# Graph propagation with residual LayerNorm: the scaling of the degrees and of z moved from VectorE to GpSimd

## The reference, cut to what matters

```python
# x: (8, 2048, 64), W = adj: (8, 2048, 2048), U: (2048, 16), w_scale: scalar
Ws = 0.5 * (W + swapaxes(W, -1, -2))
A = sigmoid(U @ U.T)
K = Ws * A
deg = maximum(K.sum(axis=-1), 1e-12)
d = rsqrt(deg)
y = w_scale * einsum('bnm,bmc->bnc', K * d[:, :, None] * d[:, None, :], x)
out = layernorm(x + y)
```

## Time and profile before

| | |
|---|---|
| median of 3 runs | 464.87 us (460.85 to 467.07) |
| the profiled execution's own time | 463.4 us |
| its span in the trace | 461.6 us |
| PE busy | 433.8 us, 94% |
| DVE busy | 412.7 us, 89% |
| ACT busy | 207.8 us, 45% |
| POOL busy | 116.8 us, 25%, 134 instructions |
| one batch, steady | about 52.4 us |

### The profile page before, as it was taken

The page is one execution under the profiler, slowest core; times in us unless marked ns, Lnnn a source line. Parts: engine busy times, 40 slices in busy tenths (PEclk is TensorE's granted clock), DMA queues, the critical chain, the costliest instruction groups (busy, mean ns, idle before and its releaser), DMA issues.

```text
span 461.6 us, 14416 instructions
## 1 busy us (share of the span) xinstructions
PE 433.8 (94%) x5302; PEld 227.9 (49%) x5302; DVE 412.7 (89%) x1153; ACT 207.8 (45%) x655; POOL 116.8 (25%) x134
## 2 busy tenths in 40 slices
PE   7887999999998999999999999999999999999993
PEld 6555444554444544554445544554445544555341
DVE  6988777999899988999899989999899998999645
ACT  3797332654254433553426442554426543454311
POOL 0000000013340334203340234203340234303444
PEclk9999899999999999999999999999999999999997
DMA  8999699988999799998999999998999999996012
GB/s 284 387 315 389 223 381 355 350 286 313 369 350 304 277 364 355 372 282 324 383 340 354 316 328 342 389 284 322 386 338 357 325 318 343 386 285 232 2 43 49
DMA packets 101386, 143.09 MB, mean 310 GB/s; under 512 B 35824, under 2 KB 35824, under 8 KB 101360
## 3 DMA queue, kind: packets, MB, share of 16 engines
q1 hardware_dynamic: 86496, 139.01, 85.7%
q10 hardware_dynamic: 14864, 3.74, 4.2%
HBM read 138.54 MB, written 4.19 MB: 309 GB/s over the span
## 4 chain that ended last, share of the span: by engine, by line
PE 81%; DVE 7%; ACT 6%; issue 3%; DMA 2%; POOLq 0%; POOL 0%; DVEq 0%; SPq 0%
PE yp L449 46%; PE kt L407 15%; PE tw L407 15%; ACT k L574 3%; DVE k L691 2%; DVE k L680 2%; ACT gate L561 2%; PE yp L550 2%; PE yp L469 2%; DMA k<-in_adj_dram 1%; PE yp L482 1%; DMA h<-in_L_gnn_U_dram 1%; PE kt L493 1%; DVE ut_a L671 0%; DVE var L739 0%
## 5 line engine op out<-in xcount | busy, mean ns | idle before, releaser
L574 ACT ACTIVATE k<-kt 128x512 f32<-128x512 f32 (+3 forms) x288 | 149.3, 523 | 222.6 <-PE kt L407 222.5
L449 PE MATMUL yp<-k,z 128*64 128x512 f32 x960 | 239.0, 611 | 0.0
L680 DVE TENSOR_TENSOR k<-tw,k 128x512 f32<-128x512 f32 (+2 forms) x320 | 193.3, 604 | 22.3 <-PE tw L407 17.9
L691 DVE CUSTOM_DVE_ANT_0 k<-k,gate 128x512 f32<-128x512 f32 (+2 forms) x320 | 196.1, 613 | 0.0
L407 PEld LDWEIGHTS tw<-ident,k 64*128 64x128 f32 x2176 | 80.6, 139 | 79.7 <-issue 74.4
L407 PEld LDWEIGHTS kt<-ident,k 64*128 64x128 f32 x1920 | 73.7, 139 | 62.4 <-issue 48.8
L407 PE MATMUL kt<-ident,k 64*128 64x64 f32 x1920 | 91.6, 228 | 13.0 <-ACT k L574 11.7
L407 PE MATMUL tw<-ident,k 64*128 64x64 f32 x2176 | 98.6, 228 | 2.9 <-issue 1.5
L449 PEld LDWEIGHTS yp<-k,z 128*64 128x64 f32 x960 | 56.5, 136 | 66.6 <-issue 55.3
L329 POOL TENSOR_TENSOR d<-deg,minus_half 128x4 f32<-128x4 f32 x32 | 32.4, 1012 | 197.6 <-DVE deg L701 197.6
L574 ACT ACTIVATION_READ_ACCUMULATOR k<-kt 128x1 f32 x288 | 57.2, 199 | 0.0
(11 more groups left out here) (54 smaller groups left out, 130.2 us busy)
## 6 DMA issues: line engine op xcount, KB each, us to landing
k<-in_adj_dram SPq DMA_DIRECT2D x128, 1024.0 KB, 7.3
xt<-in_x_dram ACTq DMA_DIRECT2D x7, 512.0 KB, 9.0
out_dram<-h SPq DMA_DIRECT2D x7, 512.0 KB, 9.5
xt<-in_x_dram SPq DMA_DIRECT2D x1, 512.0 KB, 14.0
out_dram<-k SPq DMA_DIRECT2D x2, 128.0 KB, 2.1
out_dram<-k SPq DMA_DIRECT2D x3, 64.0 KB, 1.7
h<-in_L_gnn_U_dram SPq DMA_DIRECT2D x1, 128.0 KB, 3.3
out_dram<-k ACTq DMA_DIRECT2D x1, 64.0 KB, 1.9
```

Of the source, the lines that this page charges most:

```text
L449: t = pe.matmul(yp[at:at + C, m // 2, :], z[:, n * G + c, :], K[(n, m)][:, c, :], start=(q == first_unit[m] and c == 0), stop=(q == last_u ...
L574: nc.scalar.activation(K[(j, i)][:, r, c0:UW].rearrange("p (c h e) -> p c h e", h=2, e=H), whole_rows(kt[:, 0:2, :], r % 2, (UW - c0) // P ...
L680: nc.vector.tensor_tensor(row, whole_rows(tw[:, tw_bank[g] // 2 * 2:tw_bank[g] // 2 * 2 + 2, :], g % 2, w // P), row, ALU.add).then_inc(su ...
L691: nc.vector.tensor_tensor_reduce(row, row, A[:, A_AT[g]:A_AT[g] + w], 1.0, 0.0, ALU.mult, ALU.add, deg_parts[:, i * G + r, j:j + 1]).then_ ...
```

## The change

POOL makes all three small steps of a group in a row: it waits for DVE's sum, scales the degrees, takes the power, and multiplies x by d. DVE keeps the sum alone. POOL's part for z stands at the degrees' row (25, 32, 42, 43), where it follows the power at once. `Z_ROWS` is gone. A separate semaphore increment (`deg_taken`) stands between POOL's wait and its first instruction. `FIRST_PRODUCT_ROWS` and `FIRST_DEG_ROWS` are new names for batch 0 with the same numbers as the tables beside them.

```diff
+FIRST_PRODUCT_ROWS = [29, 29, 31, 32, 33, 33, 35, 35, 37, 37, 39, 39, 42, 44, 44, 45, 45, 45, 45, 45, 47, 47, 50, 50, 52, 54, 56, 56, 59, 61, 63, 65]
 DEG_ROWS = [25, 32, 42, 43]
-Z_ROWS = [26, 34, 43, 44]
+FIRST_DEG_ROWS = [25, 32, 42, 43]
...
             def degrees(b, k):
+                pool.wait_ge(deg_summed, NZ * b + (k + 1))
+                s = slice(*Z_GROUPS[k][:2])
+                pool.sem_inc(deg_taken, 1)
+                nc.gpsimd.tensor_scalar(deg[:, s], deg[:, s], 0.5, DEG_EPS, ALU.mult, ALU.max).then_inc(deg_ready, 1)
                 pool.wait_ge(deg_ready, NZ * b + (k + 1))
-                s = slice(*Z_GROUPS[k][:2])
                 nc.gpsimd.tensor_tensor(d[:, s], deg[:, s], minus_half[:, s], ALU.pow).then_inc(d_ready, 1)
 
+            def make_z(b, k, first):
+                pool.wait_ge(d_ready, NZ * b + (k + 1))
+                pool.wait_ge(x_loaded, b * 16 + 16)
+                if not first:
+                    pool.wait_ge(prod_done, b * NQ + (LAST_PAIR_OF_Z[k] + 1 - NQ))
+                n0, n1, _ = Z_GROUPS[k]
+                nc.gpsimd.tensor_tensor(z[:, n0:n1, :], xt[:, n0:n1, :], per_row(d, n0, n1),
+                                        ALU.mult).then_inc(z_ready, 1)
...
                 nc.vector.tensor_reduce(deg[:, n0:n1], deg_parts[:, n0:n1, :], AX_X, ALU.add).then_inc(deg_summed, 1)
-                dve.wait_ge(deg_summed, NZ * b + (k + 1))
-                nc.vector.tensor_scalar(deg[:, n0:n1], deg[:, n0:n1], 0.5, DEG_EPS, ALU.mult,
-                                        ALU.max).then_inc(deg_ready, 1)
-
-            def make_z(b, k, first):
-
-                n0, n1, _ = Z_GROUPS[k]
-                dve.wait_ge(d_ready, NZ * b + (k + 1))
-                dve.wait_ge(x_loaded, b * 16 + 16)
-                if not first:
-                    dve.wait_ge(prod_done, b * NQ + (LAST_PAIR_OF_Z[k] + 1 - NQ))
-                nc.vector.tensor_tensor(z[:, n0:n1, :], xt[:, n0:n1, :], per_row(d, n0, n1),
-                                        ALU.mult).then_inc(z_ready, 1)
```

More of the change, by code:

```diff
@@ L221, in bass_graph_resnorm_kernel @@
         banks_taken = sem("banks_taken")
-        deg_summed, deg_ready, d_ready, z_ready = sem("deg_summed"), sem("deg_ready"), sem("d_ready"), sem("z_ready")
+        deg_summed, deg_taken, deg_ready = sem("deg_summed"), sem("deg_taken"), sem("deg_ready")
+        d_ready, z_ready = sem("d_ready"), sem("z_ready")
         prod_done, y_copied, yt_done = sem("prod_done"), sem("y_copied"), sem("yt_done")
@@ L326, in degrees, with beside @@
             def degrees(b, k):
+                pool.wait_ge(deg_summed, NZ * b + (k + 1))
+                s = slice(*Z_GROUPS[k][:2])
+                pool.sem_inc(deg_taken, 1)
+                nc.gpsimd.tensor_scalar(deg[:, s], deg[:, s], 0.5, DEG_EPS, ALU.mult, ALU.max).then_inc(deg_ready, 1)
                 pool.wait_ge(deg_ready, NZ * b + (k + 1))
-                s = slice(*Z_GROUPS[k][:2])
                 nc.gpsimd.tensor_tensor(d[:, s], deg[:, s], minus_half[:, s], ALU.pow).then_inc(d_ready, 1)
+            def make_z(b, k, first):
[6 more added lines that the diff above has]
+                                        ALU.mult).then_inc(z_ready, 1)
             def beside_row(b, row):
                 pool.wait_ge(lower_done, b * NL + row)
-            def beside(b, row, lag):
+            def beside(b, row, lag, first):
                 for k in range(NZ):
-                    if due(row, lag, DEG_ROWS[k]):
+                    if due(row, lag, (FIRST_DEG_ROWS if first else DEG_ROWS)[k]):
                         degrees(b, k)
+                        make_z(b, k, first)
                 for k in range(LN_PARTS):
@@ L354, in steps @@
                     for lag in range(lags - 1, -1, -1):
-                        beside(b - lag, row, lag)
+                        beside(b - lag, row, lag, lags - lag == 1)
             steps(0, 1)
@@ L363, in _ @@
                     degrees(B - 1, k)
+                    make_z(B - 1, k, False)
             for k in range(LN_PARTS):
@@ L497, in products_at @@
                 for at in range(NQ * G):
-                    if due(row, lag, PRODUCT_ROWS[at]):
+                    if due(row, lag, (FIRST_PRODUCT_ROWS if first else PRODUCT_ROWS)[at]):
                         product(b, at // G, at % G, first)
@@ L753, in beside @@
                 for k in range(NZ):
-                    if due(row, lag, DEG_ROWS[k]):
+                    if due(row, lag, (FIRST_DEG_ROWS if first else DEG_ROWS)[k]):
                         sum_degrees(b, k)
-                    if due(row, lag, Z_ROWS[k]):
-                        make_z(b, k, first)
                 if due(row, lag, SCALE_ROW):
@@ L846, in _ @@
                     sum_degrees(B - 1, k)
-                if Z_ROWS[k] >= NL:
-                    make_z(B - 1, k, False)
             for k in range(2):
```

## The result

The changed kernel takes 475.29 us in the median (474.63 to 477.46, 4 runs), the kernel before 463.59 us beside it: a ratio of 1.0247, 95% interval 1.02 to 1.0294. Now and then an execution of any of these kernels is over 1.5% slower than its fastest; the ratios and the comparisons at equal clock leave these out. The forecast was 465.5 us and no change that can be told, with a range up to 471. Run again beside other kernels (e8), the changed one gave 475.39 us and 1.0237 (1.0159 to 1.0315).

A forecast was written before the change was run, and what follows sets the result against it. PE was taken as the bound, with DVE's relief counted at nothing. z2 late by 0.07 us in each of 8 batches adds 0.6 us: 464.0 for the profiled execution, 465.5 for the median, range 460 to 471.

The forecast's parts named there:

- The scaling on POOL: Scaling of 128x4 ahead of the power: assumed 0.19 us, from a line through two plain POOL multiplications.
- The hand-offs: Waits between steps of the chain to z: 0.08 us each, 0.22 us ahead of z in the loop.
- DVE's relief: 32 scalings and 32 multiplications taken from DVE, 19.3 us of its busy time; counted as no gain.
- the chain to z: POOL's steps from the end of DVE's sum to z: 2.27 us, 2.35 until PE sees it.
- the paragraph on the shared port: DVE gate products and POOL exclude each other; no meeting with z due at z0 or z2, sum unchanged.
- The first: Rival: z2 and z0 really late through POOL's longer chain, 474 to 477 us; chance 0.17, of which 0.07 over 2%.
- The relief: Rival: PE's waits for DVE in first batches and 0.2 us per steady batch go, 460 us; chance 0.15.
- the first use: Rival: POOL's first tensor_scalar costs something once, 465.6 us by the rows or 471 by the skill; chance 0.03.
- DVE as the bound: Rival: DVE's full stretch sets PE's pace, so its relief gives 451 us, or 458 for half; chance 0.05.

The follow-up runs named there:

- e8: The changed kernel unedited, run again beside other kernels: 475.39 us, ratio 1.0237.
- e4: Changed kernel without the scaling instruction, its factor 0.5 moved into the last factor f, power and z still on POOL: 462.93 us, ratio 0.9957.
- e7: Changed kernel with one more instruction of the scaling's form and size on POOL ahead of the scaling: 472.64 us, ratio 1.0211.
- e5: Kernel before with first products of z0 at row 30 instead of 29, pair 4's at 46 instead of 45: 471.98 us, ratio 1.0153.
- e3: Changed kernel with first products of z0 at row 30 instead of 29, pair 4's at 46 instead of 45: 469.59 us, ratio 1.0108.

## Why the prediction was wrong

**Held.** PE bounds the kernel, and in the changed kernel it is a late z that lengthens the steady batch. The scaling on POOL: 0.23 us for an assumed 0.19. The hand-offs: 0.08 and 0.25 for 0.08 and 0.22. z where it is free: 0.61. z1 and z3 are hidden. DVE's relief is near nothing in the steady batches (52.28 us in e4 against 52.36), and no gain in the first three is shown to be its work.

**The step that failed** is the 1.01 us of the power in the chain to z, and with it the paragraph on the shared port. The duration was taken from a row in which the power started 0.46 us ahead of the gate product, and it was carried to a place where it starts together with it. The prediction moved the power and left DVE's gate product where it was, though the scaling that it took from DVE had stood in front of it: 0.23 us of the lost 0.46 come from each. The rule of the port was then tried on z alone, with starts worked out from an unheld power; the conclusion that at z0 and z2 no meeting was due and the sum was the same by both was wrong. The chain at z0 took 3.47 us from the end of DVE's sum (260.41 to 263.88) instead of 2.27: of the 1.20 us more, 0.56 are the held power, 0.53 the held z, and the rest the scaling and the hand-offs. z0 was not 0.20 us early but 0.99 late, and z2 not 0.07 late but about 0.6, of which 0.22 reached PE's block.

**The rule and the rows.** The Trainium skill, "SBUF — State Buffer", in "Who interferes with whom", says that a VectorE instruction with two SBUF inputs and a GpSimd one that reads SBUF exclude each other, and that issue order decides who waits. The lengths of the held powers and z agree: each is longer by the rest of the gate product, 0.53 to 0.56 us of the 0.60 up to its accumulator read, and in e7 by what was left of it. The gate product of 1.05 us behind POOL's addition agrees from the other side. Applied to the power as well as to z, the rule would have raised the question that the prediction passed over. It would not have settled it, since on two points rows and page differ. At z2 the power started 0.02 us ahead of the gate product and was the one held, so order alone does not tell who waits when both start together. And the page has the port held for the whole instruction, whereas in the kernel before and in e4 a power of 1.01 us and a gate product of 0.68 overlapped by 0.55 to 0.57 us and neither was longer.

**The rivals.** The first had the right side (late z0 and z2), but for the wrong reason: it looked for a dear scaling or a dear z by itself, and the scaling came out at 0.23 us. That its price of 9.4 to 12.1 us takes in the measured 11.7 is luck, since its mechanism is not the one found and the late z explains only part of the 11.7. The chance of 0.07 for over 2% was too low, as was the bound of the range, which allowed for unknown durations of the new instructions and none for the old one. The relief, the first use (the first scaling, at 47.85, took 0.23 us like the others) and DVE as the bound did not happen.

**The size.** About 5.4 us is the price of the mechanism by e7's profile; the four steady intervals alone give 4.7. In the changed kernel's profile the rest of the 10.9 us of span goes with the clock: 3.2 us behind waits for z, and 2.4 us that are left of the late start in batch 3. The medians of the runs do not bear this out in full. At equal mean clock they stay further apart than 5.4 us: 22 runs of the kernel before beside the experiments had a granted clock of 0.970 to 0.983 and took 463.9 to 467.9 us (median 465.6), and the seven of the changed kernel in that band took 473.0 to 477.5 (median 474.7). Its eighth, at 0.987, took 475.9. So of the 11.7 us between the medians, 2.6 go with the lower mean clock as the kernel before shows it, and 9.1 do not. One possible reason, not tested, is that the same mean can hide a fall at a dearer place. Why no run of the changed kernel reached 0.990 stays open too.

## What to carry to other kernels

When a step is put ahead of an instruction on POOL, its neighbours on DVE change too: before taking an old duration, look at what DVE does in the instant where the instruction will now start, and count a hold of up to the rest of a two-SBUF-input instruction for each POOL instruction in the chain. Relieving the neighbour moves its instructions as well: half of the lost distance came from DVE. Judge parts of a change by the steady batch and not by the ratio alone: the scaling alone stood at 1.003 and looked harmless, while the power was already held and a batch cost 0.8 us more. z on POOL was free by itself; with both, z was held as well and a batch cost 1.2. And test a remedy on the kernel before as well: e5 showed that e3's edit costs more than it hides.

## What the runs showed of the hardware

A POOL power on 128x4 that starts 0.43 to 0.59 us ahead of a gate product of DVE is not held and does not hold it (at z1, 0.17 us ahead of one of 128 columns, neither); started with it or 0.02 us ahead, it is longer by nearly the whole gate product (1.57 us beside one of 0.68, 1.44 beside one of 0.54). A reading that fits these rows is that it needs SBUF at its start only; this was not tried by itself. A gate product of 384 columns that starts 0.09 us behind POOL's addition of x takes 1.05 us instead of 0.55. A tensor_scalar on 128x4 takes POOL 0.23 us, so of the power's 1.01 most is its operation. z held by a gate product took 1.14 us instead of 0.61.
